# Attention diagonals computed once and divided by DVE and GpSimd work, with the attention output kept transposed, in an adaLN transformer block

## The reference

```
h = layernorm(x) * (1 + ca) + sa
q = h @ W_q ; latent = (h @ W_k + h @ W_v) @ W_down_kv
k = latent @ W_up_k ; v = latent @ W_up_v            # 16 heads of 16
scores = q k^T / 16 * exp(-0.01 * |t_q - t_k|)        # 1024 x 1024 for each batch and head
attn = softmax(scores) ; out = attn @ v
x = x + ga * (out @ W_o)
h = layernorm(x) * (1 + cb) + sb
x = x + gb * fp4_linear(silu(fp4_linear(h, w_gate)) * fp4_linear(h, w_up), w_down)
```

## Time and profile before

| | |
|---|---|
| time of 3 runs | 2753.26 us median, 2751.92 to 2756.32 |
| the profiled execution | 2753.01 us, its span 2751.1 us |
| mean granted TensorE clock | 0.944 of full speed |
| projection stage and setup | 0 to about 349 us |
| attention stage | about 349 to 2062 us |
| feed-forward setup and stage | about 2062 to 2751 us |
| busy over the span | PE 94%, DVE 84%, ACT 58%, POOL 35% |

### The profile page before, as it was taken

The page is one execution under the profiler, slowest core; times in us unless marked ns, Lnnn a source line. Parts: engine busy times, 40 slices in busy tenths (PEclk is TensorE's granted clock), DMA queues, the critical chain, the costliest instruction groups (busy, mean ns, idle before and its releaser), DMA issues. The chain is left out here.

```text
span 2751.1 us, 44454 instructions
## 1 busy us (share of the span) xinstructions
PE 2592.5 (94%) x15110; PEld 1205.3 (44%) x15110; DVE 2308.7 (84%) x4659; ACT 1600.6 (58%) x2988; POOL 971.2 (35%) x865
## 2 busy tenths in 40 slices
PE   5787669999999999999999999999977999999998
PEld 3333304344344344344344344343323566666665
DVE  5988788888888888888888888888755888888886
ACT  3666507777777777777777777777762222222221
POOL 3666532222122122122122122122131565556664
PEclk9667659999999999999999999999996999999999
DMA  4778864546546536446446446456201111111110
GB/s 153 239 243 257 264 127 82 85 62 91 82 62 92 81 66 95 74 69 96 72 71 95 70 74 95 69 74 92 47 7 39 37 44 42 41 41 43 41 34 18
DMA packets 207074, 238.20 MB, mean 87 GB/s; under 512 B 32256, under 2 KB 150784, under 8 KB 206720
## 3 DMA queue, kind: packets, MB, share of 16 engines
q1 hardware_dynamic: 194560, 218.56, 41.2%
q0 software_dynamic: 3072, 8.39, 1.2%
q10 hardware_dynamic: 9216, 8.39, 0.9%
HBM read 149.79 MB, written 83.89 MB: 85 GB/s over the span
## 5 line engine op out<-in xcount | busy, mean ns | idle before, releaser
L856 DVE CUSTOM_DVE_ANT_0 unread<-max_ps,toeplitz_sb 128x1024 bf16<-128x1024 f32 x1024 | 1218.5, 1218 | 212.9 <-PE max_ps L689 207.6
L817 ACT ACTIVATE probs<-score_ps 128x512 f32<-128x512 f32 x2048 | 1111.5, 598 | 431.0 <-PE score_ps L722 287.3
L689 PE MATMUL max_ps<-k_low,q_low 96*128 96x512 bf16 x2048 | 712.9, 391 | 27.5 <-DVE ident_bf L847 17.9
L651 POOL TENSOR_TENSOR probs<-probs,up_probs 128x512 f32<-128x512 f32 x256 | 336.3, 1314 | 610.0 <-ACT up_probs L821 610.0
L750 PE MATMUL pv_ps<-probs,v 128*32 128x512 f32 x4096 | 545.5, 605 | 3.3 <-POOL probs L651 3.3
L714 PE MATMUL score_ps<-q_up,k_up 99*128 99x512 bf16 (+3 forms) x1280 | 408.6, 320 | 5.3 <-ACT probs L817 4.5
L722 PE MATMUL score_ps<-q_low,k_low 99*128 99x512 bf16 (+3 forms) x1280 | 406.2, 318 | 5.2 <-ACT probs L817 4.5
L1284 PE MATMUL gu_ps<-wgu_t,turned 128*128 128x512 f32 (+1 forms) x768 | 314.4, 559 | 0.6 <-DVE hid L1445 0.6
L657 POOL DMA_DIRECT2D attn<-out_n x64 | 48.8, 763 | 694.8 <-DVE out_n L920 671.4
L714 PEld LDWEIGHTS score_ps<-q_up,k_up 99*128 99x128 bf16 x1280 | 123.8, 97 | 357.3 <-ACT probs L817 340.8
L689 PEld LDWEIGHTS max_ps<-k_low,q_low 96*128 96x128 bf16 x2048 | 193.3, 99 | 146.0 <-DVE row_max L856 68.3
(11 more groups left out here) (145 smaller groups left out, 3186.3 us busy)
## 6 DMA issues: line engine op xcount, KB each, us to landing
splits<-parts SPq DMA_DIRECT2D x128, 384.0 KB, 2.7
q_low<-splits SPq DMA_DIRECT2D x192, 128.0 KB, 4.4
k_low<-splits SPq DMA_DIRECT2D x192, 128.0 KB, 7.2
q_up<-splits SPq DMA_DIRECT2D x192, 128.0 KB, 9.8
k_up<-splits SPq DMA_DIRECT2D x192, 128.0 KB, 12.7
v_padded<-v_out SPq DMA_DIRECT2D x64, 256.0 KB, 3.7
v<-v_padded SPq DMA_DIRECT2D x32, 512.0 KB, 14.8
x_in<-in_L_attn_x SPq DMA_DIRECT2D x16, 512.0 KB, 5.3
```

The costliest lines, as they stand in the source:

```text
L651: nc.gpsimd.tensor_tensor(probs[:, g % PROBS, :, at:at + P], probs[:, g % PROBS, :, at:at + P], up_probs[:, g % 2], ALU.add).then_inc(diag ...
L689: mm = pe.matmul(max_ps[:, i % 2, half * HALF:(half + 1) * HALF], low[0][u][0:KROWS, h, qb * P:(qb + 1) * P], low[1][u][0:KROWS, h, half * ...
L817: nc.scalar.activation(probs[:, g % PROBS, h, :], score_ps[:, i % 2, :], ACT.Exp).then_inc(exp_done, 1)
L856: nc.vector.tensor_tensor_reduce(unread[:, i % 2, :], max_ps[:, i % 2, :], toeplitz[:, at:at + S], 1.0, -3.0e38, ALU.mult, ALU.max, row_ma ...
```

## The change

1. The diagonal block is made once. `diagonals` multiplies the low stacks without the three rows of the maximum into `side_ps`, one step ahead of its use. DVE multiplies it by a constant 128x128 decay (`decay_diagonal`), GpSimd subtracts the maximum (`shift_diagonal`, from a buffer `shift` in which the maxima are spread over all partitions), and ACT takes the exponential straight into `probs` (`diagonal_exp`). The products of L718 and L719 and the addition of L651 are gone, and ACT's exponential skips the block where it lies at an edge of the tile.
2. The maxima also go to DRAM whole and come back spread over 128 partitions: `max_whole` (16 KB) is stored and loaded twice a unit as 1 MB (`load_shift`).
3. The output stays transposed. `turn_out` and the two DVE steps are gone. The four rows of sums are stored to DRAM and loaded as 128x16 (`turn_sums`), inverted by DVE (`invert`, in steps 10 and 15), stored and loaded again with each row repeated 32 times (`spread_inverse`, 256 KB), and GpSimd multiplies (`normalise`). The stores (`store_out`, four of 32 KB for each half) go to SP's queue.
4. `v` has two buffers, and its load waits for the last use of the one before. Some scratch buffers share memory.
5. In the feed-forward stage the attention output is loaded transposed; `turn_attention` is gone, ACT copies half as much, and the pipeline is one tile shorter.

```diff
@@ attend_stage, SP's list
         def load_max_rows(unit, u):
-            sp.wait_ge(max_turn_copied, unit + 1)
+            sp.wait_ge(max_turn_copied, 2 * (unit + 1))
...
+            if unit > 0:
+                sp.wait_ge(shift_loaded[1], 16 * unit)
+            sp.dma_start(t["max_whole"], max_whole[:]).then_inc(max_stored, 16)
+
+        def load_shift(unit, hf):
+            sp.wait_ge(max_stored, 16 * (unit + 1))
+            if unit > 0:
+                sp.wait_ge(diag_shifted, 2 * DIAG * (unit - 1) + DIAG * (hf + 1))
+            sp.dma_start(shift[:, hf], t["max_whole"].rearrange("(h c) q -> h (c q)", c=TILES)[
+                :, hf * HALF:(hf + 1) * HALF].unsqueeze(0).broadcast_to([P, UH, HALF])).then_inc(shift_loaded[hf], 16)
+
+        def turn_sums(unit, hf):
+            n = 2 * unit + hf
+            sp.wait_ge(out_copied, n + 1)
+            sp.dma_start(t["sums"][hf], out_t[HD:P:VW, n % OUTS, :]).then_inc(sums_stored[hf], 16)
+            sp.wait_ge(sums_stored[hf], 16 * (unit + 1))
+            sp.dma_start(sums[:, hf, :], t["sums"][hf].rearrange("h (a c) -> (h a) c", a=P // UH)
+                         ).then_inc(sums_loaded[hf], 16)
+
+        def spread_inverse(unit, hf):
+            sp.wait_ge(inverted[hf], unit + 1)
+            sp.dma_start(t["inverse"][hf].rearrange("h (a c) -> (h a) c", a=P // UH), inverse[:, hf, :]
+                         ).then_inc(inverse_stored[hf], 16)
+            if unit > 0:
+                sp.wait_ge(out_normal[hf], unit)
+            sp.wait_ge(inverse_stored[hf], 16 * (unit + 1))
+            sp.dma_start(inverse_rows[:, hf, :], t["inverse"][hf].unsqueeze(1).broadcast_to(
+                [UH, VW, HALF])).then_inc(inverse_loaded[hf], 16)
+
+        def store_out(unit, hf):
+            b, u, n = unit // UNITS, unit % UNITS, 2 * unit + hf
+            sp.wait_ge(out_normal[hf], unit + 1)
+            for h in range(UH):
+                sp.dma_start(t["attn_t"][b, u * UH + h, :, hf * HALF:(hf + 1) * HALF],
+                             out_t[h * VW:h * VW + HD, n % OUTS, :]).then_inc(out_stored[n % OUTS], 16)
...
                 load_up(b if u < UNITS - 1 else b + 1, (u + 1) % UNITS)
+            if unit > 0:
+                load_shift(unit, 1)
+                sp.wait_ge(pv_done, STEPS * unit)
+            if not (last and u == UNITS - 1):
+                load_v(b if u < UNITS - 1 else b + 1, (u + 1) % UNITS)
+            if unit > 0:
+                spread_inverse(unit - 1, 0)
+                turn_sums(unit - 1, 1)
+                if unit > 1:
+                    store_out(unit - 2, 1)
+                store_out(unit - 1, 0)
+            turn_sums(unit, 0)
+            if not (last and u == UNITS - 1):
                 load_max_rows(unit + 1, (u + 1) % UNITS)
+                load_shift(unit + 1, 0)
+            if unit > 0:
+                spread_inverse(unit - 1, 1)
@@ GpSimd
+        def shift_diagonal(unit, g):
...
+            nc.gpsimd.tensor_tensor(diag[:, g % 2], diag[:, g % 2], shift[:, hf, :, at:at + P],
+                                    ALU.subtract).then_inc(diag_shifted, 1)
+
+        def normalise(unit, hf):
+            n = 2 * unit + hf
+            pool.wait_ge(inverse_loaded[hf], 16 * (unit + 1))
+            nc.gpsimd.tensor_tensor(out_t[:, n % OUTS, :], out_t[:, n % OUTS, :], inverse_rows[:, hf, :],
+                                    ALU.mult).then_inc(out_normal[hf], 1)
+
+        def unit_steps(unit):
+            for g in range(DIAG):
+                shift_diagonal(unit, g)
...
+                normalise(unit - 2, 1)
...
+                normalise(unit - 1, 0)
             for g in range(TILES + DIAG, STEPS):
+                shift_diagonal(unit, g)
@@ PE
             if is_diagonal(g):
-                at = score_ps[:, i % 2, turn - q0:turn - q0 + P]
-                pe.matmul(at, low[1][u][:, h, ks], low[0][u][:, h, ks], start=True, stop=False)
-                mm = pe.matmul(at, ident_bf[:], unserved[:], start=False, stop=True)
                 turn += P
...
-                mm = pe.matmul(side_ps[:, h, :], up[1][u % 2][:, h, ks], up[0][u % 2][:, h, ks],
+                mm = pe.matmul(side_ps[:, h, :], low[1][u][0:KROWS, h, ks], low[0][u][0:KROWS, h, ks],
@@ ACT
+        def diagonal_exp(b, u, g):
+            unit, at = UNITS * b + u, g % DIAG * P
+            act.wait_ge(exp_done, SCORE_TILES * unit + UH * (g + 1))
+            act.wait_ge(diag_shifted, diagonals_before(unit, g + 1))
+            nc.scalar.activation(probs[:, g % PROBS, :, at:at + P], diag[:, g % 2], ACT.Exp).then_inc(diag_exp_done, 1)
@@ DVE
+                if is_diagonal((g + 1) % STEPS) and not (last and g == STEPS - 1):
+                    decay_diagonal(*steps_on(b, u, g))
+                if g == 10 and unit > 0:
+                    invert(unit - 1, 1)
+                if g == 15:
+                    invert(unit, 0)
@@ feed_stage
-    TURN_ATTENTION = 0
-    PROJECT = NORM = 1
+    PROJECT = NORM = 0
...
-                mm = pe.matmul(out_ps[:, 0:D], turned[i % 2][:, k, :], w["wo_g"][:, b, k, :],
+                mm = pe.matmul(out_ps[:, 0:D], attn_in[i % 4][:, k, :], w["wo_g"][:, b, k, :],
```

More of the change, by code:

```diff
@@ L677, in _ @@
+        for unit in range(UNITS * B):
+            unit_steps(unit)
+        pool.wait_ge(diag_shifted, 2 * DIAG * UNITS * B)
+        normalise(UNITS * B - 2, 1)
+        pool.wait_ge(out_normal[1], UNITS * B - 1)
+        normalise(UNITS * B - 1, 0)
+        pool.wait_ge(out_normal[0], UNITS * B)
+        normalise(UNITS * B - 1, 1)
     @block.tensor
@@ L1538, in constants @@
     ahead = np.arange(TOEPLITZ)[None, :] - (S - P) - np.arange(P)[:, None]
-    before = np.arange(P)[None, :] < np.arange(P)[:, None]
-    large = np.float32(-2.0 ** 100)
-    unserved = np.where(before, large, np.float32(0))
+    behind = np.arange(P)[:, None] - np.arange(P)[None, :]
     return {
@@ L1548, in constants @@
         "toeplitz": np.exp(-2.0 * decay * np.maximum(ahead, 0)).astype(np.float32),
-        "unserved": (unserved.view(np.uint32) >> 16).astype(np.uint16),
-        "up_limit": np.where(before, np.float32(3.0e38), large),
+        "diag_decay": np.exp(-2.0 * decay * np.maximum(behind, 0)).astype(np.float32),
     }
```

316 lines of the change are left out of this document (146 added, 170 removed).

## The result

| | before | after |
|---|---|---|
| median of four runs | 2753.26 us | 2933.18 us (2926.85 to 2956.18) |
| ratio, with its 95% interval | | 1.0667 [1.0608, 1.0726] |
| span of the profiled execution | 2751.1 us | 2925.1 us |
| attention stage ends at | 2062.50 us | 2240.45 us |
| from there to the end | 688.6 us | 684.7 us |

The prediction was 2777 us with a range of 2660 to 2895: the sign and the engine that sets the pace came out, the size did not. All of the loss lies in the attention stage, 178.0 us; the last stage gives back 3.9 in this execution.

What follows compares the result with a forecast made beforehand. An attention-stage loop of PE and ACT, DVE close behind, bounds it now; then SP's list, 52.6 us a unit. 2753.0 us plus 40.6 - 2.7 - 6 + 13 - 21 = +23.9 gave 2777 us, range 2660 to 2895.

Steps and rivals of the forecast that it cites:

- The bound of now, and compute's 48 us: Attention stage: a loop of PE and ACT with DVE close behind, 51.2 us a unit now; after the change compute needs 47.9.
- SP's list becomes the pacemaker: Attention stage: SP's queue of transfers takes 52.6 us a unit, more than compute's 48 and the 51.2 before.
- The inverse's store landed at 29.0 us in the list: SP's queue: first inverse store lands 29.0 us after a unit's first load, behind v, the 1 MB shift and repeated inverse.
- 0.8 (0 to 2.7): SP's queue: delay of the first inverse's store by the repeated inverse issued just before the list, 0.8 us, at most 2.7.
- the 12.6 us in which v landed: SP's queue: v's time from issue to landing, 11.2 + 12.6 = 23.8 us after the unit's first load.
- Store of the sums behind the repeated inverse, 3.7 us: SP's queue: 256 KB repeated inverse lands in 3.5 us, sums' store behind it, so SP goes on at about 32.7.
- 2 us more in the middle of the list: SP's queue, slow-inverse rival: at a quarter of the DMA engines' rate 256 KB takes 2.7 us instead of 0.7.
- The rest of the list: SP's queue from 32.7 to 52.6 us: issues, other sums, maxima's rows and store, second shift, last repeat, wake-ups.
- The shifts at the stacks' rate: Rival, SP's queue: 6.7 us for each 1 MB shift, list 58.4 us, 2945 us; chance 0.21 shared with the slow inverse.
- The repeated inverse is slow: Rival, SP's queue: 256 KB on 4 engines, list 54.6 to 56.5 us, 2835 to 2890 us; 0.21 shared with slow shifts.
- The end of the stage, 18 us from the first sums: End of attention stage: sums, inverses, multiplication and stores follow each other, about 18 us instead of 4.9: +13.
- The last stage, -21: Feed-forward stage: PE's two transposes and ACT's shorter copy save 0.3 us in each of 64 tiles, -19; shorter pipeline -2.

## Why the prediction was wrong in size

By its own terms, with the unit shown above:

- **The bound of now, and compute's 48 us**: right. With the list out of the way, a unit takes 47.72 us (47.9 worked out), and its diagonal steps 3.03 us on average (2.98 worked out); the kernel with the diagonal part alone has 48.63.
- **SP's list becomes the pacemaker**: right, by its waits. That the list is longer than compute, too.
- **The inverse's store landed at 29.0 us in the list**: this is the step that failed. SP went on behind it at 1005.54 - 971.92 = 33.6, 4.6 later (33.7 as the mean landing of the 27 units). The mis-sized term is the "0.8 (0 to 2.7)" for the repeated inverse issued just ahead of the list: it cost 4.4. It was measured from both sides: on 16 engines this landing comes at 29.3 and a unit is 4.5 us shorter; cut to 8 KB, at 29.5 and 3.9 shorter. My upper bound was below the truth, since I took 256 KB for bytes to be moved and not for a delay of four engines that all later transfers wait for. Some 1 us more, in sum, comes from the base: the 12.6 us in which v landed are those of one unit, nearly the shortest of all, where the page of the kernel before has a median of 14.8. As the mean of the 27 units v landed at 25.9 us after the first load there and not at the 23.8 that I went on from; the first shift took back half a microsecond, 3.3 (v at 29.1 on 16 engines, 25.9 before) instead of 3.8, and the store itself some 0.4.
- **Store of the sums behind the repeated inverse, 3.7 us**: 1010.86 - 1006.17 + 0.6 = 5.3. The rival's "2 us more in the middle of the list" for a quarter of the DMA engines' rate was close: 1.6.
- **The rest of the list**: nine issues 4.1 (4.1), the other sums 2.1 (2.4), six rows 3.8 (3.7), maxima 1.7 (1.9), second shift and store 5.7 (6.3), the last repeat 0.7 (0.5), and no wake-ups (1.0). Together 1.8 less than I had. The sum of all is 52.6 + 4.6 + 1.6 - 1.8 = 57.0.
- **The shifts at the stacks' rate** (6.7 us each): falls. The second moves at 344 GB/s in the window above, and both together cost 5.9 us of the list by the run without them, where this rival had 13.4.
- **The repeated inverse is slow**: this rival was the true one. It said 2835 to 2890 us for a list of 54.6 to 56.5; the list has 57.0 and the time is 2933. Its bound for that delay of the stacks, 1.9 us, was too low as well.
- **The end of the stage, 18 us from the first sums**: 2240.45 - 2221.51 = 18.9, right.
- **The last stage, -21**: -3.9 (-1.4 in the kernel with the same last stage that gained least). PE's two transposes give 9.62 - 9.40 = 0.22 us a tile, not 0.3, and of that DVE's longer `normed` let 0.07 through. "PE is the bound there with 96%, so it counts in full" was the false step: DVE had only 1.1 us of idle time in a tile (266 of 300 us busy), and the end of a GpSimd product that it had just met so far.
- **The sum**: units 31 x 5.73 = +178 where the prediction had +32 for all of them; the rest of the attention stage +0.4, since the last group of the maxima's rows now goes out later in its unit's compute (61.1 us from it to the first store of sums at the end, 73.7 to the last transposes before) and that balances the longer end of the stage; the last stage -3.9. Together the span's 174.0.

The theory that survives all runs: SP's list waits for landings in the order of the list, and the landing of a small store comes after the bulk loads ahead of it on the same queue. It is supported from four sides: less in the rings (51.5), the slow transfer spread (52.9), half of the list gone (48.6 and 50.3, then at compute's pace), and the same transfers without a wait behind them (47.7). Why the unit's length scatters from 49.0 to 59.9 us in the changed kernel was not tested, and it says nothing on what small stores wait for on a second queue.

## What to carry to other kernels

A small transfer here cost its own 1.5 to 1.9 us only on an empty ring; behind the bulk loads it cost 20 us, to whoever waits for it and to all that is queued behind the waiter. Issue the small store first, then the bulk, then the reader: here that order (with DVE's inversion of one half three steps later) turned +6.7% into -3.5%, and moving the same waits to another queue made it worse (2963 against 2933 us). When a term is taken from one row of a trace, look at the median of its group too: v's 12.6 us were 14.8. Before a change is dropped, try its parts: both halves of this one were gains, and only their sum overran the list.

When an engine that had been the bound is relieved, look at how late the next engine's inputs may be, and which instruction of the other engines it will now start beside.

## What the runs showed of the hardware

- A 256 KB load that goes to 128 partitions but has four rows as its source ran on a quarter of the DMA engines (share 0.23, 87 GB/s), and with it the last stack that was issued behind it landed 4.9 us later and v 4.4 us later than with the same bytes as four DMAs of 64 KB. With those the last stack landed as in the kernel before, 24.8 us after the first load.
- A 1 MB load of a 16 KB source repeated onto 128 partitions in pieces of 2 KB moved at 344 GB/s in a window of 1 us, more than twice the 152 GB/s of the stacks, in pieces of the same size onto 16 partitions for each load.
- GpSimd waited up to 17.7 us for an 8 KB store on its own queue while bulk loads ran on SP's, and up to 10.6 us with the repeated inverse spread over all engines.
- A DVE instruction of 404 ns (128x256, f32, SBUF to SBUF) took 944 ns when it started 0.8 us before the end of a GpSimd product, ending 0.15 us after that did; started 0.12 us before the end it took 404 ns. One of 0.89 us with an input in PSUM took 0.89 beside the same product.
- After PE had been idle for 6.9 us its granted clock was 0.50 in the window 1010 to 1015 us, and a product of 384 columns took 0.53 us at 1014.21, where it took 0.34 at 1006.57.
